# Both layer norms applied by ScalarE as scale and shift, and slot buffers three deep, in a fused attention and mixture-of-experts kernel

## The reference

```
h = concat(tokens(x), txt)                       # 32 x 165 x 256
h = h + attention(layernorm(h))                  # 16 heads of 16, causal, every 4th key column masked
h = h + moe(layernorm(h))                        # below
layernorm(x) = (x - mean) / sqrt(var + 1e-5)     # no gain, no bias
```

## Time and profile before

| | |
|---|---|
| Median of 3 runs | 918.27 us |
| The profiled execution: its own time | 917.84 us |
| Its span (first to last instruction) | 916.1 us |
| Mean granted TensorE clock | 0.909 of full speed |
| Busy: PE, DVE, ACT, POOL | 758.9, 609.1, 354.0, 374.2 us |
| Chain that ended last | PE 25%, DVE 10%, issue 4%, DMA 3%, POOL 2%, ACT 1% of the span |

### The profile page before, as it was taken

One profiled execution on the slowest core, in us unless ns is written; L12 is line 12 of the kernel. 1 busy time (PEld: TensorE's weight loads), 2 busy tenths in 40 slices (PEclk: granted clock), 3 DMA queues, 4 the chain that ended last, 5 costly groups with the idle time before them and its releaser, 6 DMA issues. The chain is left out here.

```text
span 916.1 us, 18658 instructions
## 1 busy us (share of the span) xinstructions
PE 758.9 (83%) x6840; PEld 685.4 (75%) x6840; DVE 609.1 (66%) x1439; ACT 354.0 (39%) x761; POOL 374.2 (41%) x440
## 2 busy tenths in 40 slices
PE   4898999999999999999996213588989898988994
PEld 3677788787788887788874212588989898988994
DVE  1337787787787787687675588676768585766551
ACT  0204433343334343334331252264545546454560
POOL 3014534543543553443532330334353635444344
PEclk8899999999999999999997555599989898989897
DMA  9955556756645755456741611104324342432122
GB/s 291 266 77 84 78 90 103 114 91 94 86 89 98 113 97 89 86 88 92 111 71 36 212 46 47 31 23 84 122 31 126 43 121 49 113 83 30 30 31 31
DMA packets 80686, 82.35 MB, mean 90 GB/s; under 512 B 36162, under 2 KB 74944, under 8 KB 80245
## 3 DMA queue, kind: packets, MB, share of 16 engines
q1 hardware_dynamic: 67980, 66.92, 37.3%
q0 software_dynamic: 11584, 10.96, 7.6%
q10 hardware_dynamic: 1032, 3.30, 1.0%
HBM read 34.59 MB, written 16.22 MB: 55 GB/s over the span
## 5 line engine op out<-in xcount | busy, mean ns | idle before, releaser
L579 POOL DMA_INDIRECT out<-r_arena x48 | 79.9, 1664 | 124.1 <-DVE r_arena L1516 113.7
L647 ACT ACTIVATE r_arena<-ps_all 126x660 f32<-126x660 f32 x128 | 92.2, 720 | 85.5 <-PE ps_all L849 85.3
L504 POOL TENSOR_SCALAR_AFFINE_SELECT r_arena<-r_arena 126x660 f32<-126x660 f32 x128 | 97.6, 768 | 55.8 <-ACT r_arena L647 55.8
L1232 DVE RECIPROCAL r_arena<-ps_all 128x165 f32<-128x165 f32 x64 | 76.1, 1189 | 57.5 <-PE ps_all L864 57.5
L1221 DVE TENSOR_REDUCE mx<-ps_all 128x4 f32<-128x504 f32 (+1 forms) x160 | 104.3, 665 | 10.0 <-PE ps_all L826 8.2
L1081 PE MATMUL ps_all<-xeT_hi,W_hi 128*128 128x330 f32 x256 | 88.6, 346 | 26.6 <-DVE hT_lo L1538 26.6
L566 POOL DMA_INDIRECT xe<-xn_rows,r_arena x48 | 69.2, 1443 | 86.2 <-DVE r_arena L1507 51.5
L1538 DVE TENSOR_TENSOR hT_lo<-r_arena,hT_hi 128x330 fp32r<-128x330 f32 x128 | 62.6, 501 | 52.0 <-ACT r_arena L730 44.9
L728 ACT ACTIVATE hT_hi<-ps_all,vec_s 128x330 fp32r<-128x330 f32 x128 | 68.8, 537 | 69.6 <-PE ps_all L1081 61.1
L826 PE MATMUL ps_all<-Kp,Qp 96*65 96x56 f32 (+1 forms) x512 | 90.4, 293 | 0.0
L849 PE MATMUL ps_all<-Qp,Kp 98*126 98x166 f32 x512 | 85.1, 290 | 4.0 <-ACT r_arena L647 2.7
(11 more groups left out here) (174 smaller groups left out, 1715.7 us busy)
## 6 DMA issues: line engine op xcount, KB each, us to landing
H<-w SPq DMA_DIRECT2D x16, 1024.0 KB, 5.5
Qp<-q_hi SPq DMA_DIRECT2D x64, 166.0 KB, 4.0
Kp<-k_hi SPq DMA_DIRECT2D x128, 63.0 KB, 4.2
Qp<-q_lo SPq DMA_DIRECT2D x32, 166.0 KB, 4.6
out<-H SPq DMA_DIRECT2D x16, 330.0 KB
xn_rows<-r_arena SPq DMA_DIRECT2D x16, 330.0 KB
Kp<-k_lo SPq DMA_DIRECT2D x64, 63.0 KB, 4.2
H<-h SPq DMA_DIRECT2D x1, 3360.0 KB, 23.3
```

Of the source, the lines that this page charges most:

```text
L504: pool.affine_select(PT[0:S, g, :, :], PT[0:S, g, :, :], [[0, 4], [STEP - 1, T]], ALU.is_ge, 0.0, base=STEP - 2, channel_multiplier=-STEP) ...
L579: pool.indirect_dma_start(rows_out, bass.IndirectOffsetOnAxis(tok[0:A, u, a:a + 1], 0), yw[0:A, a, :], None, bounds_check=NTOK - 1, comput ...
L647: act.activation(PT[0:S, g, :, :].rearrange("p (k h) t -> p k h t", k=2), pair[:, :, :, 0:T], ACT.Exp, scale=float(HD) ** -0.5).then_inc(e ...
L1232: dve.reciprocal(rS[:, c, :], bank(2 + c)[:, T:2 * T]).then_inc(rs_sum, 1)
```

## The change

Two things are done.

**Layer norms.** ACT applies both norms, as `Identity(scale * x + bias)` with a scale and a bias per row: the scale is `rs`, the bias is the new `shift` = -mean * rs. POOL makes `shift` with two more small instructions per norm (110x3 each): -mean after `vv`, and the product with `rs` after the power. `ln1_apply(n + 2)` moves from the odd round to the even round before it; `ln2_apply(n - 1)` stays in its odd round. In ACT's list both stand between `exps(b, 1)` and `copy_v(b + 2)`. `ln1_apply(0)` becomes ACT's first instruction after its first DMA issues.

**Slot buffers.** `slotv`, `tokf`, `tok` and `wslot` have three buffers (`NTB = 3`), so `tokens(e + 1)` waits for the scatter of expert e - 2 instead of e - 1. POOL's loop over the middle experts, which was a loop with registers over pairs of experts, is written out; the order of its DMAs is the same.

The diff, without declarations, renamed arguments and the removed functions' bodies:

```diff
-        R_ARENA = sb("r_arena", [128, 8520])
+        R_ARENA = sb("r_arena", [128, 8576])
-        slotv = cut(R_ARENA, 2, NV, NA)
-        tokf = cut(R_ARENA, 2, NA)
-        tok_w = cut(R_ARENA, 2, NA)
+        slotv = cut(R_ARENA, NTB, NV, NA)
+        tokf = cut(R_ARENA, NTB, NA)
+        tok_w = cut(R_ARENA, NTB, NA)
...
 @@ POOL, rstd1 (scale2 is changed in the same way)
                 pool.tensor_scalar(vv[0:A, :], mv[0:A, :, 1], EPS, 1.0, ALU.add, ALU.mult).then_inc(rs1_chain, 1)
-                pool.wait_ge(rs1_chain, n + 1)
+                if n >= 1:
+                    pool.wait_ge(xn1_ready, RT * n)
+                    apart(pool)
+                pool.tensor_scalar(shift[0:A, :], mv[0:A, :, 0], -1.0, 0.0, ALU.mult, ALU.add).then_inc(rs1_chain, 1)
+                pool.wait_ge(rs1_chain, 2 * n + 2)
                 apart(pool)
                 pool.tensor_tensor(rs[0:A, :], vv[0:A, :], kf("minus_half")[0:A], ALU.pow).then_inc(rs1_ready, 1)
+                pool.wait_ge(rs1_ready, n + 1)
+                apart(pool)
+                pool.tensor_tensor(shift[0:A, :], shift[0:A, :], rs[0:A, :], ALU.mult).then_inc(shift1_ready, 1)
...
 @@ POOL, after the functions gather(e) and scatter(e)
-            gather(0, 0)
-            regather(1, 1)
-            scatter(0, 0, False)
-            with pool.Fori(0, NE // 2 - 1) as it:
-                regather(2 * it + 2, 0)
-                scatter(2 * it + 1, 1, True)
-                regather(2 * it + 3, 1)
-                scatter(2 * it + 2, 0, True)
-            scatter(NE - 1, 1, True)
+            gather(0)
+            for e in range(1, NE):
+                pool.wait_ge(xet_done, 4 * e)
+                apart(pool)
+                gather(e)
+                scatter(e - 1)
+            scatter(NE - 1)
...
 @@ ACT
+            def ln1_apply(n):
+                act.wait_ge(shift1_ready, n + 1)
+                if n >= 1:
+                    act.wait_ge(t1_done, 2 * n)
+                for r in range(RT):
+                    act.activation(xn1[0:A, r, :], H4[0:A, n, r, :], ACT.Identity, bias=shift[0:A, r:r + 1],
+                                   scale=rs[0:A, r:r + 1]).then_inc(xn1_ready, 1)
+            def ln2_apply(p):
+                act.wait_ge(shift2_ready, p + 1)
+                if p >= 1:
+                    act.wait_ge(xn2_ready, RT * p)
+                for r in range(RT):
+                    act.activation(xc[0:A, r, :], H4[0:A, p, r, :], ACT.Identity, bias=shift2[0:A, r:r + 1],
+                                   scale=rs2[0:A, r:r + 1]).then_inc(xc_ready, 1)
+            ln1_apply(0)
...
                     exps(b, 1)
+                if u == 0 and 0 < n + 2 < NPAIR:
+                    ln1_apply(n + 2)
+                if u == 1 and 0 <= n - 1 < NPAIR:
+                    ln2_apply(n - 1)
                 if 0 <= b + 2 < B:
                     copy_v(b + 2)
...
 @@ DVE (ln1_stats_of and ln2_stats_of also wait for shift1_ready and shift2_ready of the pair before)
                 if u == 0 and n + 2 < NPAIR:
                     ln1_stats_of(n + 2)
-                if u == 1 and n + 2 < NPAIR:
-                    ln1_apply(n + 2)
                 if u == 1 and has_p:
                     ln2_stats_of(n - 1)
...
                     row_max(b + 1, 2)
-                if u == 1 and has_p:
-                    ln2_apply(n - 1)
                 if has_r:
                     row_max(b + 1, 3)
...
-            def tokens(e, u, again):
+            def tokens(e):
+                u = e % NTB
 
                 dve.wait_ge(idx_done, e + 1)
-                if again:
-                    dve.wait_ge(scattered, 16 * NA * (e - 1))
+                if e >= NTB:
+                    dve.wait_ge(scattered, 16 * NA * (e - NTB + 1))
```

More of the change, by code:

```diff
@@ L47 @@
 HALF = CAP // 2
+NTB = 3
 STEPS, DIGIT, NCAND, ONACT = 10, 8, 7, 3
@@ L159, in build @@
         rs, rs2 = sb("rs", [128, RT]), sb("rs2", [128, RT])
+        shift, shift2 = sb("shift", [128, RT]), sb("shift2", [128, RT])
         L = sb("L", [128, NT, NE])
@@ L566, in gather, with scatter @@
                     pool.indirect_dma_start(xe[0:A, a, :], None, xn_rows,
-                                            bass.IndirectOffsetOnAxis(tok[0:A, u, a:a + 1], 0),
+                                            bass.IndirectOffsetOnAxis(tok[0:A, e % NTB, a:a + 1], 0),
                                             bounds_check=NTOK - 1).then_inc(gathered[a // 3], 16)
             rows_out = out.rearrange("b t d -> (b t) d")
-            def scatter(e, u, again):
+            def scatter(e):
                 for a in range(NA):
@@ L1161, in stats @@
                     dve.bn_aggr(m[0:A, r, :], s[0:A, r, :]).then_inc(ready, 1)
[L1163 to L1166, removed]
             def ln1_stats_of(n):
@@ L1507, in tokens, with weigh @@
                 dve.tensor_copy(tok[0:A, u, :], tokf[0:A, u, :]).then_inc(tok_ready, 1)
-            def weigh(e, u, tiles, again):
+            def weigh(e, tiles):
                 for a in tiles:
@@ L1513, in weigh @@
                     dve.wait_ge(yt_done, NA * e + (2, 2, 3, 5, 5, 6)[a])
-                    if again and a == 0:
+                    if e > 0 and a == 0:
                         dve.wait_ge(scattered, 16 * NA * e)
-                    dve.tensor_scalar(yw[0:A, a, :], bank(at_bank)[0:A, at_col:at_col + D], wslot[0:A, u, a:a + 1],
+                    dve.tensor_scalar(yw[0:A, a, :], bank(at_bank)[0:A, at_col:at_col + D], wslot[0:A, e % NTB, a:a + 1],
                                       None, ALU.mult).then_inc(y_ready, 1)
@@ L1552, in hidden, with expert @@
                        .then_inc(w2_split, 1)
-            def expert(e, u, seen, more, again):
+            def expert(e, u, seen, more):
                 v = 1 - u
@@ L1563, in expert @@
                     low_hidden(0, range(5, 2 * SV_AT_FIRST + 2))
-                    tokens(1, 1, again)
+                    tokens(1)
                     low_hidden(0, range(2 * SV_AT_FIRST + 2, 2 * KFF))
@@ L1567, in expert @@
                     hidden(e, u, seen, range(0, 1))
-                    weigh(e - 1, v, range(3, NA), e > 1)
+                    weigh(e - 1, range(3, NA))
                     hidden(e, u, seen, range(1, SV_AT + 1))
-                    tokens(e + 1, v, again)
+                    tokens(e + 1)
                     hidden(e, u, seen, range(SV_AT + 1, KFF))
@@ L1577, in expert @@
                     one_hot_places(e + 2, range(0, 1))
-                weigh(e, u, range(0, 3), again)
+                weigh(e, range(0, 3))
                 low_xeT(e + 1, range(2, 4))
@@ L1595, in _ @@
             for e in range(NE - 1):
-                expert(e, e % 2, 16 * (e // 2) + 16, e + 2 < NE, e > 0)
+                expert(e, e % 2, 16 * (e // 2) + 16, e + 2 < NE)
             hidden(NE - 1, 1, 8 * NE, range(0, 1))
-            weigh(NE - 2, 0, range(3, NA), True)
+            weigh(NE - 2, range(3, NA))
             hidden(NE - 1, 1, 8 * NE, range(1, KFF))
             dve.wait_ge(tok_chain, 4 * NE)
-            weigh(NE - 1, 1, range(NA), True)
+            weigh(NE - 1, range(NA))
 def kernel(**inputs):
```

40 lines of the change are left out of this document (19 added, 21 removed).

## The result

The changed kernel takes 858.71 us (median of 4 runs, 855.88 to 860.04), the kernel before 918.03 us (4 runs beside it, 917.41 to 920.11): the ratio is 0.9346, with a 95% interval of 0.9317 to 0.9375. Forecast were 860.5 us, in a range of 853 to 873. The profiled execution took 859.55 us (before 917.84), with a span of 857.7 us (before 916.1).

A forecast was written before the change was run, and what follows sets the result against it. PE, busy 83% of the span, was held up by waits for DVE and then slowed by its clock. From 917.84, 38.4 (part 1) and 19 (part 2) were taken: 860.4, called 860.5 us; range 853 to 868, or 873 with unknown costs.

The forecast's parts named there:

- Part 1: Experts, third slot buffer: six stops removed, 24.3 us, and slow matmuls behind them, 14.1; sum 38.4 us, 33 to 40.
- The clock term: Experts, fc1's last 48 matmuls: without stops they run as in expert 0; 5 x 2.48 + 1.70 = 14.1 us.
- Part 2: Attention, norms off DVE: PE's waits for row maxima shrink; 18.6 us, called 19, range 8 to 27.
- the terms for the rounds: Attention rounds: 23.4 us of stops removed, less 2.8 for new stops and 1.0 for round 29.
- new small stops: Odd rounds, third exps behind the norm and POOL's last future-zeroing: 0.2 us in each of 14, 2.8 us lost.
- The fit: Odd round, ACT's list: shift ready at 243.8, V copy ends 245.9, third exps due 246.1; fits by 0.2 us.
- The tail: Rounds 31 and 33: later shift and ACT's slower start delay PE about 0.5 us each, 1.0 us back.
- The start: Program start: first norm leaves DVE's queue, but the second pair's `moved` and the load queues decide; 0.
- A: Rival, odd rounds: ACT and POOL become the bound, norms gain only 4 us; 875 us, chance 0.11.
- B: Rival, attention rounds: transfers become the bound, half the norms' gain is lost; 870 us, chance 0.07.
- C: Rival, experts: another tokens input or the gathers stop DVE or PE, half of 38.4 gone; 880 us, chance 0.05.
- D: Rival, slower than before: late shift holds third exps on ACT in all rounds; 930 at 3 us late, chance 0.02.

The follow-up runs named there:

- slots_only: Kernel before with only the third slot buffer and POOL's loop written out; DVE applies both norms: 880.12 us, 0.9605.
- norms_only: Changed kernel, three buffers included, with the old wait of tokens for the scatter of expert e - 1 put back: 899.68 us, 0.9806.
- start_dve: Changed kernel with the first norm of the first two pairs of rows applied by VectorE: 857.51 us, 0.9351.
- ends_dve: start_dve with the second norm of the last two pairs applied by VectorE as well: 856.07 us, 0.9338 to the kernel before.
- tokens_at2: Kernel before, two buffers, with tokens one eighth of the hidden layer later in VectorE's order: 900.67 us, 0.9836.
- late1: Changed kernel with one more power between GpSimd's power and product in both norms, shift 1.03 us later: 885.35 us, 0.9636.
- ends_short: ends_dve with GpSimd's power for the second norm no longer waiting for the minus-mean: 855.74 us, 0.9316 to the kernel before.
- first_noshift2: first_only without GpSimd's two unread instructions for the second norm's shift and their waits: 879.08 us, 0.9565 to the kernel before.
- second_only: Changed kernel with the first norm applied by DVE again, the second by ACT: 869.12 us, 0.9448.
- first_only: Changed kernel with the second norm applied by DVE again, the first by ACT: 902.45 us (three executions), 0.9807.
- late3: Changed kernel with three more powers between GpSimd's power and product in both norms, shift 3.1 us later: 958.65 us, 1.0431.

## Why the prediction was right

**Part 1, forecast 38.4 us, measured 37.7** in the experts. The mechanism is shown from both sides: the buffers without the norms remove the stops (`slots_only`), the wait alone restores them (`norms_only`). Its two terms hold: six stops are gone, and so are the slow matmuls behind them, 39.2 together, less 1.5 for the half clock that expert 0 now has at its start. `slots_only` has that spell without a norm on ScalarE (8.79 us for the 48 matmuls), `start_dve` and `ends_dve` have norms on ScalarE and not the spell (7.40 and 7.42), so the norms are not its cause.

**The clock term, 14.1 us,** was worked out from slow matmuls of experts with a stop against expert 0, and not from the wait alone, which would have given 24.3. `tokens_at2` shows why it has to be taken separately: it is not in proportion to the stop.

**Part 2, forecast 18.6 us, measured 23.2** (24.1 in the rounds, less 0.9 in the tail). From the first query product of round 0 (66.18 and 68.72 us) to the last transposes of the maxima (478.01 and 456.45) it is 411.8 against 387.7, 24.1 less, where the terms for the rounds came to 23.4 - 2.8 - 1.0 = 19.6. The term that was mis-sized is the 2.8 us for new small stops, 0.2 in each of 14 rounds: by the waits ScalarE stopped TensorE once, for 0.2. The fit that the prediction worked out came true almost to the tenth. It had the shift ready at 243.8 and the third exps due at 246.1, which is 5.3 and 7.6 us into that round; they are at 5.43 and 7.65. `late1` shows that the room is small, since a delay of 1.03 us comes through whole where the clock stays full, and `ends_short` that a shorter chain gives nothing. Odd rounds went from 15.00 to 13.30, 1.70 less: that is the 2.05 of three stops, less 0.17 that stays and 0.08 more of TensorE's busy time, to 0.1. The two norms' shares add up where the clock is full: 0.97 for the first (15.00 to 14.03 in `first_noshift2`), 0.72 for the second (to 14.28 in `second_only`). Another 1.4 us come from round 23 of before, 16.38 us long with half clock in it, and some of the rest from round 29, where before half clock fell too.

**Prices.** One apply on ScalarE 590 to 592 ns against 569: two rows of other instructions, added up, were 4% low. The product took 0.19 us. No row had shown that, so the value taken was a good guess.

**The tail, forecast 1.0 us more, measured 0.9:** from those transposes to the last router product it is 31.5 us before and 32.4 after. In round 33 TensorE's stop for GpSimd's `norm_weight` is 6.77 for 6.00. In round 31 its stops of 0.81 and 2.64 have become one of 4.03, because the third exps stand behind the norm; some 0.4 us of that come back, since the clock is full again sooner in the matmuls behind it.
```profile
466.70 1.58 ACT L680 ACTIVATE r_arena<-H,shift,rs 110x256 f32<-110x256 f32 x3 [2.54 <-POOL shift L489]
468.19 0.70 ACT L656 ACTIVATE r_arena<-ps_all 126x660 f32<-126x660 f32 x1
```
The selection behind it takes 80.7 us in both kernels.

**The start, forecast 0:** the first query product of round 0 came at 68.7 us for 66.2. In the other kernels it was 64.8 to 72.1, and 72.1 in `ends_short`, which has no norm on ScalarE there, so the 2.5 us can't be put down to the change.

**The rivals.** A (ScalarE or GpSimd becomes the bound) did not come, but lies within 1 us of the kernel. B (transfers) is there, but small: the weight loads' wait for the maxima's DMA grew from 0.9 us to 2.0, and the matmuls stood 0.7 for it where no such wait was before. C: no new stop in fc1. D needs some 3 us of delay. The sum was 860.4 against 859.55, and that it is so close is in part luck: the rounds gave 4.5 us more than their terms, and the start (2.5) and expert 0 (1.5) took most of it back.

**Where I was wrong** was in the expectations, not in the forecast: `first_only`, `late1` and `late3` (by 32, 10 and 23 us) fell by one step, a stop priced at its own length and no clock with it; in `first_only` the longer apply, 0.47 us a round, comes on top.

## What to carry to other kernels

A wait for a transfer that an engine takes in front of others' work can cost its length and slower matmuls behind it; take both from the trace, by the same matmuls with and without the stop. Before moving small work from one engine to another, look at what it pushes on the engine that prepares it: half a microsecond on GpSimd moved its selects onto VectorE's first apply and cost 23 us in all (`first_only` against `first_noshift2`). Where TensorE is full in a round, as in the changed kernel's, a shorter chain on the other engines gave nothing, and a longer one cost its whole length and often the clock as well.

## What the hardware showed that I had not expected

- Half clock came behind stops far shorter than the 4 us of the experts: 0.81 us (8 of 13 odd rounds of `first_noshift2`), 1.28 (12 of 13 in `first_only`), 2.70 and 3.25 (`tokens_at2`), and in eight odd rounds of `late1` with no stop over 0.4 ahead. Each spell lasted 3.4 or 6.8 us. The Trainium skill, "TensorE: Matmul & The Clock Gate" (section "HAM oscillation"), describes a loop that pays a wait and then half clock each time; here that holds for the six stops of 4 us in the kernel before and for 12 of 13 stops of 1.28 us in `first_only`, and not for those of `tokens_at2` or `first_noshift2`.
- The same stop of 0.81 us at the same place in the round had full clock in the kernel before and half clock in another. None of these runs says why.
- An apply of 110x256 on VectorE takes 0.40 us by itself, 0.73 beside the start of GpSimd's `norm_weight` (in the kernel before too) and 0.87 when it starts early in one of GpSimd's selects.
